# A decoder layer on one core: a scale for each pair's weights from ACT's sums of squares, in place of a scan of all weights

## What is computed

```
x = x + attention(layernorm(x), w_qkv, w_out)            # 16 heads of 64, causal softmax
x = x + cross(layernorm(x), ctx, Wq, Wk)                 # softmax(q k^T) from ctx, applied to x
x = x + ffn(layernorm(x), ...)                           # 8 experts: gate, low-rank update
```

```
qkv = x @ w_qkv;  scores = q k^T / 8, causal;  out = softmax(scores) v;  return out @ w_out
```

## Time and profile before

| | us |
|---|---|
| median of three runs | 2708.12 (2706.8 to 2715.74) |
| the profiled execution, its own time | 2711.69 |
| its span | 2709.8 |
| PE, DVE, ACT, POOL busy | 2395.8, 1890.0, 780.1, 713.2 |

### The profile page before, as it was taken

The page is one execution under the profiler, slowest core; times in us unless marked ns, Lnnn a source line. Parts: engine busy times, 40 slices in busy tenths (PEclk is TensorE's granted clock), DMA queues, the critical chain, the costliest instruction groups (busy, mean ns, idle before and its releaser), DMA issues.

```text
span 2709.8 us, 37859 instructions
## 1 busy us (share of the span) xinstructions
PE 2395.8 (88%) x14389; PEld 1180.2 (44%) x14389; DVE 1890.0 (70%) x3421; ACT 780.1 (29%) x1557; POOL 713.2 (26%) x981
## 2 busy tenths in 40 slices
PE   0588888799898999979988999979989999988997
...
GB/s 174 227 179 170 170 199 200 210 148 146 145 105 126 138 145 142 146 201 139 154 118 100 143 143 145 143 197 128 160 146 107 119 145 146 142 149 185 109 78 93
DMA packets 986009, 403.97 MB, mean 149 GB/s; under 512 B 937116, under 2 KB 946332, under 8 KB 985828
## 3 DMA queue, kind: packets, MB, share of 16 engines
...
...
## 4 chain that ended last, share of the span: by engine, by line
PE 60%; DVE 19%; DMA 9%; issue 5%; ACT 3%; POOL 2%; SPq 1%; ACTq 0%; POOLq 0%; DVEq 0%
PE ps_p L538 8%; PE ps_p L540 8%; PE ps_p L539 8%; DMA r<-pn 7%; PE ps_s L538 7%; PE ps_s L539 7%; PE ps_s L540 7%; PE ps_s L583 6%; PE ps_o L608 5%; DVE pn L817 4%; DVE peak L854 2%; ACT probs L743 2%; DVE bn L822 2%; DMA qk<-in_x 2%; PE ps_s L588 1%
## 5 line engine op out<-in xcount | busy, mean ns | idle before, releaser
L1081 POOL TENSOR_SCALAR pn<-probs,rden 128x640 f16<-128x640 f32 (+7 forms) x512 | 388.9, 772 | 1294.5 <-DVE rden L866 774.2
L743 ACT ACTIVATE probs<-ps_s,low,back 128x640 f32<-128x640 f32 (+7 forms) x512 | 421.4, 826 | 887.3 <-DVE low L857 775.8
L817 DVE SCALAR_TENSOR_TENSOR pn<-probs,rden,pn 128x640 f16<-128x640 f32 (+7 forms) x512 | 474.6, 959 | 170.1 <-POOL pn L1081 170.1
L538 PE MATMUL ps_p<-r,w 128*128 128x512 f16 x1344 | 514.5, 383 | 2.6 <-DVE qk L817 2.6
L539 PE MATMUL ps_p<-r,w 128*128 128x512 f16 x1344 | 513.9, 382 | 0.0
L540 PE MATMUL ps_p<-r,w 128*128 128x512 f16 x1344 | 513.5, 382 | 0.0
L583 PE MATMUL ps_s<-qk 64*128 64x512 f16 (+3 forms) x2304 | 245.5, 339 | 118.6 <-ACT probs L743 108.6
L854 DVE TENSOR_REDUCE peak<-ps_s 128x2 f32<-128x1280 f32 (+3 forms) x128 | 241.4, 1886 | 40.5 <-PE ps_s L588 37.6
L608 PE MATMUL ps_o<-r,vn 128*64 128x512 f16 (+3 forms) x2304 | 213.2, 342 | 44.2 <-issue 43.7
L583 PEld LDWEIGHTS ps_s<-qk 64*128 64x128 f16 x2304 | 91.8, 97 | 266.3 <-ACT probs L743 156.7
L540 PEld LDWEIGHTS ps_p<-r,w 128*128 128x128 f16 x1344 | 132.3, 98 | 161.7 <-issue 5.3
...
## 6 DMA issues: line engine op xcount, KB each, us to landing
...
```

The costliest lines, as they stand in the source:

```text
L538: pe.matmul(ps, lh, rh, start=start and k == ks[0], stop=False)
L743: act.activation(probs_part(q, j, w), ps_s[:, j, scores(q)], ACT.Exp, bias=low[:, n % 2, i:i + 1], scale=sc, accum_out=den[:, n % 2, i:i + ...
L817: dve.scalar_tensor_tensor(out=to, in0=bank, scalar=scale, in1=rounded, op0=ALU.mult, op1=ALU.subtract).then_inc(ok, 1)
L1081: pool.tensor_scalar(to, src, scale, 1.0, ALU.mult, ALU.mult).then_inc(ok, 1)
```

## The change

- The scan of w_qkv is gone. For each pair and kind ACT takes, over the loaded block, the sums of squares of each partition (`WN`: Square with an accumulated sum, output thrown away). `WC`: PE transposes the three sums (three f32 transposes into `ps_o`), DVE takes the greatest and halves its exponent, which gives a power of two for each pair and kind, and the scale `sc(n)` of the pair's exponentials (`own_scales`).
- The rounding of the weights (`WH`) and of w_out (`VH`) moves from POOL to ACT; the rest stays with DVE, at other places.
- `WI` loads into three buffers, one for each kind (two slots of `w_raw` and half of `xn3`); for pair 0 and the value weights of pair 1 into `r3`.
- x of batch 0 has eight slots, in `x1` (r2); no AI of batch 0 waits.
- w_out: ACT also sums the squares of its eight blocks and, once more loaded, of the value weights of pairs 4 to 7 (`SN`, twelve, in pairs 0 and 1), since v and w_out share one range (`out_scales`, in pair 2); each block of w_out has its own scale (`VF`).
- In the start, PE does the first half of q, k and v, then the second halves; the constants of the experts (`CS`, `SC0`, `CF`) move behind the first halves.

```diff
-    X5 L40 L41 R5 WL0++ CL10+ L50 X6 OL0 L51 R6 CL11+ L60 L61 X7 WL1++ R7 CL20+
+    X5 L40 L41 R5 CL10+ X6 OL0 WC++ L50 L51 R6 WL0++ CL11+ L60 L61 X7 WL1++ R7 CL20+
...
-    E00 E01 CH21 E10 E11 E20 E21 CH00+ E30 E31 OH1- E40 E41 CH01+ E50 E51 CH10+ OH0 E60 E61 CH11+ E70 E71
-    CH20+
+    E00 E01 CH21 WH2+ E10 E11 WN0++ E20 E21 CH00+ WN1++ E30 E31 OH1- E40 E41 CH01+ WN2++ E50 E51 CH10+ OH0 E60 E61
+    WH0++ CH11+ E70 E71 WH1++ CH20+
 """
 POOL_BODY = """
-    WH2+ H00 H01 H10 H11 H20 H21 H30 H31 H40 H41 WH0++ H50 H51 H60 H61 WH1++ H70 H71
+    H00 H01 H10 H11 H20 H21 H30 H31 H40 H41 H50 H51 H60 H61 H70 H71
 """
 SP_BODY = """
-    WD2+ T0 T1 WS2+ WI1++ T2 T3 T4 WD0++ T5 WS0++ WI2++ T6 WS1++ WI0+++ WD1++ T7 V+
+    WD2+ WI0++ T0 WS1+ T1 WI1++ T2 WS2+ WI2++ T3 T4 WD0++ T5 T6 WS0++ WD1++ T7 V+
...
-    CS SC0 SC1 P000+ P001+ P002+ P003+ P010+ P011+ P012+ P013+ SC2 P100+ P101+ P102+ P103+ P110+ P111+ P112+ P113+
-    SC3 P200+ P201+ P202+ P203+ P210+ P211+ P212+ P213+ S0+ S1+
+    WC+ P000+ P001+ P002+ P003+ P100+ P101+ P102+ P103+ P200+ P201+ P202+ P203+ CS SC0 P010+ P011+ P012+ P013+
+    P110+ P111+ P112+ P113+ WC++ P210+ P211+ P212+ P213+ S0+ S1+
 """
 DVE_START = """
-    AB0+ AB1+ CS SR00 SR01 AL0+ AB2+ SR02 AL1+ AB3+ SR03 AL2+ AB4+ SR04 AL3+ AB5+ SR05 AL4+ AB6+ SR06 AL5+ AB7+
...
+    AB0+ AB1+ AL0+ AB2+ AL1+ AB3+ AL2+ AB4+ AL3+ WC+ AB5+ AL4+ WL0+ AB6+ AL5+ WL1+ AB7+ AL6+ WL2+ CL00+ AL7+ CL10+
+    CS CL20+ SC0 CF CL01+ CL11+ WC++ CL21+ WL0++ WL1++
...
-    AX0+ AX1+ AX2+ AX3+ AX4+ AX5+ AX6+ AX7+ CH00+ CH01+ CH10+ CH11+ CH20+ CH21+
+    AX0+ AX1+ AX2+ WN0+ AX3+ WN1+ AX4+ WN2+ AX5+ WH0+ AX6+ WH1+ AX7+ WH2+ CH00+ CH10+ CH20+ CH01+ WN0++ WN1++ CH11+
+    WN2++ CH21+ WH0++ WH1++
 """
 POOL_START = """
-    AS0+ AS1+ AH0+ AH1+ AS2+ AH2+ AS3+ AH3+ AS4+ AH4+ AS5+ AH5+ AS6+ AH6+ AS7+ AH7+ WH0+ WH1+ WH2+ WH0++ WH1++
+    AS0+ AS1+ AH0+ AS2+ AH1+ AS3+ AH2+ AS4+ AH3+ AS5+ AH4+ AS6+ AH5+ AS7+ AH6+ AH7+ CF
 """
 SP_START = """
-    AI0+ AI1+ CS SI00 SI01 SI02 AI2+ AT0+ SI03 AI3+ AT1+ SI04 AI4+ AT2+ SI05 AI5+ AT3+ SI06 AI6+ AT4+ SI07 AI7+ AT5+
-    WI0+ SI10 SI11 AT6+ AT7+ SI12 SI13 SI14 SI15 SI16 SI17 WI1+ SI20 SI21 SI22 SI23 SI24 SI25 SI26 SI27 WI2+
-    WS0+ WI0++ WS1+ WI1++ WS2+ WI2++ WS0++ V+ WI0+++ WS1++
-"""
+    AI0+ AI1+ WI0+ AI2+ WI1+ AI3+ WI2+ AI4+ AI5+ AT0+ AI6+ AT1+ AI7+ AT2+ CS AT3+ AT4+ AT5+ AT6+ AT7+ WI0++ WI1++
+    WI2++ WS0+ WS1+ WS2+ WS0++ V+
...
 ONCE = {
-    ("SP", 0, "T1"): "SI30 SI31 SI32 SI33", ("DVE", 0, "R6"): "SR30 SR31 SR32 SR33",
-    ("SP", 1, "T1"): "SI34 SI35 SI36 SI37", ("DVE", 1, "R6"): "SR34 SR35 SR36 SR37",
-    ("DVE", 2, "R1"): "SM4", ("PE", 2, "M0"): "SC4", ("DVE", 2, "R6"): "SC4",
+    ("DVE", 2, "R1"): "SM", ("PE", 2, "S5"): "SC1", ("DVE", 2, "X5"): "SC1",
 }
+for pair, first in ((0, 0), (1, 6)):
+    for at, row in (("T0", (0, 1, 2)), ("T4", (3,)), ("T5", (4,)), ("T6", (5,))):
+        ONCE["SP", pair, at] = " ".join(f"SI{first + e:02d}" for e in row)
+    for at, row in (("E31", (0,)), ("E41", (1,)), ("E51", (2,)), ("E61", (3,)), ("E71", (4, 5))):
+        ONCE["ACT", pair, at] = " ".join(f"SN{first + e:02d}" for e in row)
+for pair in range(3, 7):
+    u, v = 2 * pair - 6, 2 * pair - 5
+    ONCE["SP", pair, "T0"] = f"VI{u}"
+    ONCE["DVE", pair, "R1"] = f"VF{u}"
+    ONCE["ACT", pair, "E41"] = f"VH{u}"
+    ONCE["DVE", pair, "R4"] = f"VL{u}"
+    ONCE["SP", pair, "T4"] = f"VI{v}"
+    ONCE["ACT", pair, "E71"] = f"VH{v}"
+    ONCE["SP", pair, "T5"] = f"VS{u}"
+    ONCE["DVE", pair, "R7"] = f"VL{v}"
+    ONCE["SP", pair, "T7"] = f"VS{v}"
...
+        def turn_of(n, t, h):
+
+            return 6 * n + (3 * h + t if n == 0 else 2 * t + h)
+
+        def proj_bank(n, t, h):
+            return ps_s[:, 0, half(turn_of(n, t, h) % 2)] if n % PAIRS == 0 else ps_p[:, h, :]
+
+        def raw(n, t):
+
+            if n == 0 or n == 1 and t == 2:
+                return first_raw[:, 3 if n else t, :]
+            return w_raw[:, t, :] if t < 2 else xn3[:, 1, :]
+
+        def x_in(T):
+            return x1[:, T, :] if T < TB else c_probs[:, T % 2, :]
+
+        def junk(n):
+
+            return pt[:, 8 * SEQ:9 * SEQ].rearrange("p (t d) -> p t d", t=TB) if n < 2 else o16[:, :, 0, PAIRS - 1, :]
+
+        def sum_of(n, t):
+            c = 8 * t + n if n < 4 or t < 2 else 32 + n - 4
+            return squares[:, c:c + 1]
...
-                        if k >= 2:
-                            sp.wait_ge(w_ok, k - 1)
-                        sp.dma_start(w_raw[:, k % 2, :], w_qkv[k].rearrange("p u c d -> p (u c d)")
-                                     ).then_inc(w_in[k % 2], 16)
+                        if n >= 3 or n == 2 and t < 2:
+                            sp.wait_ge(w_ok, 3 * n + t - 2)
+                        sp.dma_start(raw(n, t), w_qkv[3 * n + t].rearrange("p u c d -> p (u c d)")).then_inc(w_in[t], 16)
...
+                        e = 10 * a[0] + a[1]
+                        if e >= 3:
+                            sp.wait_ge(scan_ok, e - 2)
+                        sp.dma_start(wo_scan[e % 3], w_out[e] if e < 8 else
+                                     w_qkv[3 * (e - 4) + 2].rearrange("p u c d -> p (u c d)")).then_inc(scan_in[e % 3], 16)
...
+                        if b > 0:
+                            if i < 2:
+                                sp.wait_ge(n_lo, TB * b)
+                            else:
+                                sp.wait_ge(a_lo, T - 1)
+                        sp.dma_start(x_in(T), x[b, i]).then_inc(a_in[T % 2] if b > 0 else a_first[i], 16)
...
+                    elif kind == "WC":
+                        if n >= PAIRS:
+                            return
+                        pe.wait_ge(own_ok, 3 * n + 3)
+                        if n == 0:
+                            pe.wait_ge(set_cst, 2)
+                        else:
+                            pe.wait_ge(own_up, n)
+                        if n >= 3:
+                            pe.wait_ge(o_ok, 2 * n - 4)
+                        if n == 4:
+                            pe.wait_ge(grp_ok, 2)
+                        for t in range(3):
+                            mm = pe.transpose(ps_o[:, 1, block_of(t)], sum_of(n, t).broadcast_to([P, P]), ident[:, :])
+                        mm.then_inc(own_turn, 1)
...
+                    elif kind == "WH":
+                        t, = a
+                        if n >= PAIRS:
+                            return
+                        act.wait_ge(own_up, n + 1)
+                        if n > 0:
+                            act.wait_ge(part_ok, 4 + t if n == 1 else 6 * n + 2 * t - 4)
+                            act.wait_ge(w_st[t], 16 * n)
+                        act.activation(w16[:, t, 0, :, :].rearrange("p c d -> p (c d)"), raw(n, t), ACT.Copy,
+                                       scale=scale(n, t)).then_inc(wh_ok, 1)
+                    elif kind == "WN":
+                        t, = a
+                        if n >= PAIRS:
+                            return
+                        act.wait_ge(w_in[t], 16 * (n + 1))
+                        if n + t > 0:
+                            act.wait_ge(own_ok, 3 * n + t)
+                        act.activation(junk(n), raw(n, t).rearrange("p (t d) -> p t d", t=TB), ACT.Square, scale=NORM,
+                                       accum_out=sum_of(n, t)).then_inc(own_ok, 1)
                     elif kind == "E":
...
+                    if kind == "SN":
+                        e = 10 * a[0] + a[1]
+                        act.wait_ge(scan_in[e % 3], 16 * (e // 3 + 1))
+                        if e > 0:
+                            act.wait_ge(scan_ok, e)
+                        act.activation(o16[:, :, 1, PAIRS - 1, :], wo_scan[e % 3].rearrange("p (t d) -> p t d", t=TB), ACT.Square,
+                                       scale=NORM, accum_out=scan_sum(e)).then_inc(scan_ok, 1)
...
+                    if kind == "VH":
+                        act.wait_ge(wo_in, 16 * (i + 1))
+                        act.wait_ge(up_o_ok, i // 2 + 1)
+                        if i >= 2:
+                            act.wait_ge(wo_st[i % 2], 16 * (i // 2))
+                        act.activation(wo16[:, i % 2, 0, :], wo_raw, ACT.Copy, scale=up_o[:, i:i + 1]).then_inc(woh_ok, 1)
...
+                def own_scales(n):
+                    c = 3 * n
+                    dve.wait_ge(own_turn, n + 1)
+                    powers(slice(c, c + 3), (ps_o[:, 1, 0:3 * P], True), own_step, 4 * n)
+                    dve.tensor_scalar(up_w[:, c:c + 3], inverse[:, :], 2.0 ** 13, None, ALU.mult)
+                    dve.tensor_scalar(sc(n), power[:, c:c + 1], power[:, c + 1:c + 2], 2.0 ** -15, ALU.mult,
+                                      ALU.mult)
+                    dve.drain().then_inc(own_up, 1)
+                    dve.wait_ge(own_up, n + 1)
...
-                    if kind == "WH":
-                        t, = a
-                        k = 3 * n + t
-                        if n >= PAIRS:
-                            return
```

(19 more changed lines are left out.)

268 lines of the change are left out of this document (127 added, 141 removed).

## The result

| | before | with the change |
|---|---|---|
| median, us | 2709.14 (4 runs, the three above among them) | 2752.51 (2747.75 to 2756.78, 4 runs) |
| ratio, 95% interval | | 1.0156 (1.0129 to 1.0182) |
| profiled execution; span | 2711.69; 2709.8 | 2755.05; 2753.1 |

A forecast was written before the change was run, and what follows sets the result against it. TensorE, busy 88% of the span, was taken as the bound, with room only in the first slices. From 2711.69, -53 + 98 = +45 gives 2756.7; the median 3.6 lower is 2753 us, range 2715 to 2788.

The forecast's parts named there:

- Term 1: Start, up to pair 0's first exponential: 137.4 us falls to 84, -53 us, bounds -43 to -60.
- the hole: Start, second halves: PE's scale transposes for pair 1 wait for ACT's third sum of squares, 3 us.
- POOL's 1.1 more on eight tiles: Start: POOL's scale chain could take 1.1 us more a tile, bounding the start's gain at -43.
- Term 2: Pairs 0 to 5 of batch 0: ACT waits for late weight loads, 423 us against 325.4, +98 us.
- The sum's lower bound of 1.2: ACT's sum of squares in a pair: 1.4 us expected, at least 1.2, perhaps 2 with a strided output.
- The term of -2.5: Pair 5, to block 0 of the next pair: extra transposes and scale chain, less DVE and POOL work, -2.5 us.
- The third load, forecast at +0.7: Pair 5: load behind block 2's turn and a store, 6.5 us to landing, delays block 5 by 0.7 us.
- unchanged within 2: Pairs 6 and 7, which have no squares: no change beyond 2 us.
- A: Rival, pairs: squares only fill ACT's idle time and loads never decide; 2699 or 2665 us; chance 0.13.
- B: Rival: chain real, but landings near 3.9, tails hidden and start wins 60; +13, 2721 us; chance 0.12.
- the tails of pairs 0 and 1: Ends of those pairs, last two w_out squares: 9.8 us each; hiding them would save 13 us.
- C: Rival, pairs: loads queue, 8 us instead of 4.7 twice a pair; +40, 2793 us; chance 0.13.

The follow-up runs named there:

- e6: e3 with POOL again rounding the q, k, v weights (w_out's rounding stays on ACT): 2687.97 us, 0.9909.
- e7: e3 with two slots for x of batch 0 and SP's start order changed to match, still no scans: 2703.74 us, 0.9962.
- e1: The changed kernel with only ACT's second sum of squares moved, from before block 3's exponentials to behind block 4's: 2708.02 us, 0.9982.
- e4: e3 with the loads for w_out's sums earlier, and the start's third sum of squares ahead of an evacuation: 2674.67 us, 0.986.
- e5: e4 with weight roundings and rests moved off the pair's end, second and third weight loads behind block 0's turn: 2644.34 us, 0.9753.
- e8: e5 with the raw weight loads back behind the turns where the change had them, sums of squares still late: 2652.22 us, 0.9787.
- e3: The changed kernel with the second weight load ahead of block 0's turn and all three sums of squares one place later: 2680.81 us, 0.989.
- e2: The changed kernel with only SP's second weight load moved, ahead of block 0's turn: 2709.16 us, 0.9988.

## Why the prediction was right

**Term 1, the start: forecast -53, measured -57.6,** inside its bounds (-43 to -60). The beat is the one worked out, 5.0 us a tile where 5.1 stood: in the changed kernel's chain of waits one rest starts at 9.79 and the next at 14.78 (shown under e6):
```profile
9.79 1.23 DVE probs L1106
```
The steps were right in kind, the last weight among the last tiles included (its rest ends at 48.4 for 48.0). The first exponential came at 79.8 for 84, and the 4 us are all behind the first halves: the second halves begin at 56.9 for 58.8; their first 48 matmuls take 10.5 for 12.1, as none of them ran at the lower clock, for which the sum had 1.7; and the hole, with its transposes, is 2.1 for 3. The working has one slip that changes nothing: POOL's 1.1 more on eight tiles is 9 us, so the bound is -44 and not -43. e7 shows what part of the gain the slots have.

**Term 2, the pairs: forecast +98, measured +99.5.** Pair 5 step by step, from its first exponential:

| step | forecast | measured |
|---|---|---|
| first load landed | +14.4 | +15.9 |
| sum of squares | 1.4 | 1.06 + 0.19 |
| second load landed | +26.6 | +26.7 |
| PE's block 4 | +29.8 (14.7 later than before) | +29.4 (14.2 later) |
| its idle time | all of 14.7 | 13.79 |
| block 4's scores to block 5's exponentials | +0.7 | +0.2 |
| from there to the last block's | -2.5 (to block 0 of the next pair) | -0.2 |
| the last block's to the next pair's first | +3.3 | +3.6 |
| sum, with the 53.7 of before | 69.9 | 71.5 |

The mechanism was the one forecast, wait by wait; that the sum lies within 2 us of it owes something to luck, as errors of opposite sign cancel. The first load's issue ended 3.0 us later than worked out: a store of w_out (0.6) stood ahead of the turn of the values, the turn took 3.55 and not 1.99, and the issue 1.22 for 0.43. It landed sooner after: 3.2 us from the issue's end (449.1 less 445.9), 4.4 from its start, where 4.7 stood from the end. The times of the earlier trace rows are counted from the issue's start, so that the forecast had counted each issue twice. From the first landing to the second it then takes 10.7 us for 12.2, with a landing of 4.1 from the start and a sum of 1.06 for 1.4. So the first landing came 1.5 late, and the second on time. The first wait was 10.58 for 8 to 9, the second 7.78 for 6. The sum's lower bound of 1.2 didn't hold (1.06), and its upper one of 2, for a strided output, stands on no row: the sums of the start write without a stride and take 1.04 to 1.06, as much as the others.

The term of -2.5 for the DVE and POOL work taken out behind block 5 came and was lost again. Block 6 follows block 5 by 6.5 us for 8.5 before, but block 7 follows block 6 by 11.9 for 10.1. It does so by 11.9 in pairs 2 to 5 of e1 to e4 as well, where one or both of the waits for loads are gone, so the waits don't make it. The rows put it to DVE's order, though no version moved the scale chain to test that: between block 6's bias and its reciprocals DVE now takes the scale chain and both rests of block 5, where before one of the rests stood ahead of the peaks, and no scale chain at all. POOL, which needs the reciprocals to round block 6, stands for them, and block 7's peaks stand behind those rests:
```profile
483.03 0.23 DVE L938 TENSOR_SCALAR low<-peak,sizes 128x2 f32<-128x2 f32 x1
...
483.77 0.55 DVE L967 TENSOR_REDUCE c_peak<-ps_o 128x3 f32<-128x384 f32 x1
...
485.45 1.95 DVE L895 SCALAR_TENSOR_TENSOR pn<-probs,rden,pn 128x768 f16<-128x768 f32 x2 [0.20 <-DVEq L986]
487.32 0.16 DVE L944 TENSOR_SCALAR den_s<-den 128x2 f32<-128x2 f32 x1
```
```profile
487.77 2.96 POOL L1185 TENSOR_SCALAR pn<-probs,rden 128x896 f16<-128x896 f32 x2 [6.63 <-DVE rden L947]
```
From the start of block 6's exponentials (483.30) to these reciprocals it takes 4.0 us, before 2.3 (446.73 to 449.03). The forecast had the scale chain's 1.4 in this term, but as work to be set against other work, not as time on the way to block 7.

The third load, forecast at +0.7, made ACT wait 5.3 us, and cost 0.2: ACT had waited 7.9 us there before, for the bias.

Pairs 0 and 1 came at 65.5 and 78.9 for 68 and 76, again with errors of opposite sign. Pair 6 had +2.3 where "unchanged within 2" stood: its end takes 6.5 us for 5.2, and its block 4 comes 2.0 later behind block 3. In e5 it is 50.7, but in e6, which leaves w_out's rounding at the pair's end, it is 51.0, so that rounding doesn't explain it; what does isn't shown.

**The rivals.** A asked that ACT's idle time hide the squares: it had 172.3 us of it, but the squares stood where their loads had not landed. e5 and e8 are near A's world, made by moving the sums and roundings: there the six pairs cost 324.5 and 327.0 for 325.4 before. So A's premise (ACT has time) was true, and its conclusion needed a different order. B's premise came: the twelve loads for which ACT stood landed after (us from the issue's start, least, median, most)
```profile
DMA to landing us min/median/max: 3.6/4.0/7.2
```
But B's time didn't: the loads' issues came later in turn, the tails of pairs 0 and 1 weren't hidden (12.0 and 12.9 us for 5.3 and 5.2 before), and the start won 57.6, not 60. C's long landings didn't come; only one of the twelve took over 5.1.

The Trainium skill's page DMA: Bandwidth & Descriptors, whose fit the prediction weighed, gives it for transfers that GpSimd issues, and here SP issues them. From the issue's start no load landed within its 3.2; counted from the issue's end the first load of pair 5 took just that. A reader who takes it must say from where it counts.

What stays open: the tail of batch 0 with pair 7 takes 307.7 for 304.6, and did so in every version (306.8 to 308.4); none was made to find out why. Pairs 8 to 14 take 331.6 for 333.6 and give some of it back.

## What to carry to other kernels

An engine's idle time is free only for work whose inputs are there: before putting a step into a hand-written order, find the landing of its load in terms of that same engine's steps, and put it behind; here three sums and one load moved a few places turned +1.6% into -1.1% (e3), and the moves of e4 and e5 made it -2.5%. If a waiting step holds what later issues its successor's load (here ACT, DVE, SP, load, ACT), the waits add up each round. And when the largest wait goes, look for the one beneath it: the pair's end, in the table of waits from the first (36.8 us), was, with the moves that came along in e5, worth another 30 us.

## What the runs showed of the chip

- A sum of squares over 1024 columns takes 1.06 us (and 0.19 for reading the sum), less than the exponential of the same width, 1.20, which reads PSUM and writes f32.
- The issue of one DMA transpose by SP varies with what is ahead of it: in pairs 1 to 3 of the change, with no store just ahead, the values' turn takes 1.87 to 1.95 us, in pairs 4 and 5, behind a store of w_out, 3.52 and 3.55, and in pair 0, behind a store of weights, 3.27. The issue of the plain load behind it varies between 0.58 and 1.22, and not with that store (0.58 in pair 4, 1.22 in pair 5).
- The part from pair 7's first exponential to the end holds the same steps in all versions of the change. It took 2189.2 (e3), 2190.3 (e5), 2191.9 (e4), 2192.0 (e6 and e7), 2195.3 (e2), 2196.2 (e1) and 2196.3 us (e8), with 2195.5 in the change; before, it took 2196.4. Each figure is one execution, and executions of one version differ too: e3's four spread over 9.8 us. But three of e5's four agree within 0.5 (2643.97 to 2644.48), two of e8's within 0.1 (2651.34, 2651.37), and of the 7 between them only 1.3 lie ahead of pair 7. So a difference of up to 0.3% between two versions may come from where nothing was changed; what makes it wasn't found. e5 owes some 6 of its 67.8 us (of span, against before) to it; the other 61.7 lie in the part that was changed, and that e5 is faster stands without them.
